# Layer one's experts in an AdaLN kernel: first products three tiles ahead instead of two

## The reference

```python
shared = silu(xf @ w_shared1) @ w_shared2
comb = zeros((T, 8)).at[arange(T)[:, None], top_k_idx].add(top_k_probs)
for e in range(8):
    expert_out = silu(xf @ w1[e]) @ w2[e]
    routed = routed + comb[:, e:e + 1] * expert_out
x = x + gb * (shared + routed)
```

## Time and profile before

| | |
|---|---|
| Median of 3 runs | 957.22 us (955.15 to 957.28) |
| The profiled execution's own time | 956.11 us |
| Its span, first to last instruction | 954.3 us |
| Instructions | 16734 |
| Busy: PE, DVE, ACT, POOL | 838.4, 791.0, 555.4, 463.9 us |
| Mean granted TensorE clock | 0.957 of 2.4 GHz |
| Stage `experts(1)` on PE | 861.46 to 948.6 us |

### The profile page before, as it was taken

One profiled execution on the slowest core, in us unless ns is written; L12 is line 12 of the kernel. 1 busy time (PEld: TensorE's weight loads), 2 busy tenths in 40 slices (PEclk: granted clock), 3 DMA queues, 4 the chain that ended last, 5 costly groups with the idle time before them and its releaser, 6 DMA issues. The chain is left out here.

```text
span 954.3 us, 16734 instructions
## 1 busy us (share of the span) xinstructions
PE 838.4 (88%) x5486; PEld 590.4 (62%) x5486; DVE 791.0 (83%) x1749; ACT 555.4 (58%) x1225; POOL 463.9 (49%) x459
## 2 busy tenths in 40 slices
PE   4778999999999999999999889989985785688897
PEld 3556677777677767777777667746553633345555
DVE  6978999999999999999888989786679878856752
ACT  3657877777778777777867667312123382552321
POOL 2146677676776655545544434545223122424652
PEclk9979999999999999999999999999997787899999
DMA  7013443343433432222333122422204113402122
GB/s 265 29 30 109 139 132 115 114 132 117 138 113 105 137 106 68 77 81 96 103 89 89 50 84 67 150 78 79 89 34 102 31 17 52 144 0 67 56 91 78
DMA packets 52662, 87.16 MB, mean 91 GB/s; under 512 B 5824, under 2 KB 23744, under 8 KB 51808
## 3 DMA queue, kind: packets, MB, share of 16 engines
q1 hardware_dynamic: 43360, 73.50, 26.0%
q10 hardware_dynamic: 9216, 12.59, 3.6%
HBM read 70.67 MB, written 15.40 MB: 90 GB/s over the span
## 5 line engine op out<-in xcount | busy, mean ns | idle before, releaser
L616 PE MATMUL bank<-hTs,wA 128*128 128x512 bf16 x768 | 180.1, 382 | 0.5 <-DVE u L1866 0.5
L2445 POOL TENSOR_TENSOR xbuf<-xbuf,dec 128x384 f32<-128x384 f32 x64 | 53.4, 834 | 211.7 <-ACT xbuf L1338 169.6
L1866 DVE SCALAR_TENSOR_TENSOR u<-bank,chn,u 128x511 f32<-128x511 f32 (+2 forms) x192 | 142.8, 744 | 3.5
L616 PEld LDWEIGHTS bank<-hTs,wA 128*128 128x128 bf16 x768 | 75.5, 99 | 83.4 <-issue 5.0
L688 PE MATMUL bank<-wB,yb 128*128 128x256 f32 x512 | 121.1, 380 | 0.7 <-DVE acc L1822 0.7
L688 PEld LDWEIGHTS bank<-wB,yb 128*128 128x128 f32 x512 | 92.5, 190 | 11.2 <-issue 1.1
L2455 POOL TENSOR_TENSOR yb<-yv,gs 128x512 f32<-128x512 f32 x64 | 81.8, 1277 | 14.1 <-DVE yv L1893 13.9
L767 PE MATMUL bank<-Mm,xbuf 128*128 128x128 f32 x512 | 71.8, 284 | 18.7 <-DVE yv L1893 17.5
L767 PEld LDWEIGHTS bank<-Mm,xbuf 128*128 128x128 f32 x512 | 65.9, 196 | 30.1 <-issue 21.2
L1348 ACT ACTIVATE rel<-csb,cs 128x128 f32<-128x128 f32 x256 | 82.4, 416 | 0.0
L1338 ACT ACTIVATE xbuf<-bank,dtv 128x128 f32<-128x128 f32 x256 | 72.8, 372 | 14.1 <-PE bank L733 14.1
(11 more groups left out here) (277 smaller groups left out, 1854.1 us busy)
## 6 DMA issues: line engine op xcount, KB each, us to landing
csb<-csd SPq DMA_DIRECT2D x64, 256.0 KB, 3.5
wA<-in_win SPq DMA_DIRECT2D x32, 256.0 KB, 4.4
wAd<-wA ACTq DMA_DIRECT2D x32, 256.0 KB, 4.4
wA<-wAd SPq DMA_DIRECT2D x32, 256.0 KB, 3.7
wB<-in_wob SPq DMA_DIRECT2D x8, 512.0 KB, 6.0
wBd<-wB ACTq DMA_DIRECT2D x32, 128.0 KB, 4.3
wB<-wBd SPq DMA_DIRECT2D x8, 512.0 KB, 5.5
sS<-cbd SPq DMA_DIRECT2D x16, 256.0 KB, 3.4
```

Of the source, the lines that this page charges most:

```text
L616: last = nc.tensor.matmul(out, wpart(a, kt), hpart(c, kt), start=n == 0, stop=n == 5)
L1866: nc.vector.scalar_tensor_tensor(out=u[:, n % 2, d:S], in0=bank[0][:, 0:S - d], scalar=chn[:, hid, 3 - d:4 - d], in1=u[:, n % 2, d:S], op0 ...
```

## The change

Layer one's tiles get a third PSUM bank (`UP[1]` = banks 0, 2, 3) and a third buffer for SiLU's result (`Ex[:, 0, 0:3]`, a tile of the attention, in place of two buffers in `words`). PE issues products(0), (1), (2) first, and products(m + 3) where it issued products(m + 2). PE's wait for a bank and ACT's wait for a buffer are for tile m - 3. The attention's leftovers move from bank 3 to bank 4, in all the places where bank pair (1, 3) stood. Layer zero's `UP[0]` = (0, 2) gives what stood there. POOL's and SP's lists are not touched.

```diff
-                         words[:, 0:2 * S].rearrange("p (f n) -> p f n", n=S),
+                         Ex[:, 0, 0:3, :],
...
+        UP = ((0, 2), (0, 2, 3))
...
                 def products(m):
                     b, pos, f = tile(L, m)
-                    if m > 1 and L:
-                        pe.wait_ge(q["fth_done"], tiles(1, m - 2))
+                    if m > 2 and L:
+                        pe.wait_ge(q["fth_done"], tiles(1, m - 3))
+                    elif L:
+                        pass
...
                     pe.wait_ge(q["fw_done"], (FT[0] if L else 0) + pos + 1)
                     for n in range(w13n):
-                        last = split_product(bank[2 * (m % 2) + n][:, :],
+                        last = split_product(bank[UP[L][m % len(UP[L])] + n][:, :],
...
                         for kt in range(KT):
-                            turned_heads(1, kt, bank[(1, 3)[kt]]).then_inc(q["a_attT"], 1)
+                            turned_heads(1, kt, bank[(1, 4)[kt]]).then_inc(q["a_attT"], 1)
...
-                products(1)
+                ahead = len(UP[L])
+                for m in range(1, ahead):
+                    products(m)
                 pe.wait_ge(q["zb_done"], L + 1)

                 for m in range(B * nf):
                     b, pos, _ = tile(L, m)
-                    if m + 2 < B * nf:
-                        if tile(L, m + 2)[0:2] == (1, 0):
+                    if m + ahead < B * nf:
+                        if tile(L, m + ahead)[0:2] == (1, 0):
                             pe.wait_ge(q["hts_done"], 8 if L == 0 else 12)
-                        products(m + 2)
+                        products(m + ahead)
                     (heads_ended if L else second_batch)(m)
...
                 def hidden(m):
                     b, pos, _ = tile(L, m)
-                    if m > 1:
-                        act.wait_ge(q["fh_done"], hidden_tiles(L, m - 2))
+                    ring = len(UP[L])
+                    if m >= ring:
+                        act.wait_ge(q["fh_done"], hidden_tiles(L, m - ring))
...
                     act.wait_ge(q["fu"], tiles(L, m))
-                    out = room[L].fth[:, m % 2, :]
+                    out = room[L].fth[:, m % ring, :]
...
-                    nc.scalar.activation(out, bank[2 * (m % 2)][:, :], ACT.Silu).then_inc(q["fth_done"], 1)
+                    nc.scalar.activation(out, bank[UP[L][m % ring]][:, :], ACT.Silu).then_inc(q["fth_done"], 1)
...
-                    nc.vector.tensor_tensor(room[L].hf[:, m % 3, :], room[L].fth[:, par, :], other, ALU.mult).then_inc(q["fh_done"], 1)
+                    nc.vector.tensor_tensor(room[L].hf[:, m % 3, :], room[L].fth[:, m % len(UP[L]), :], other, ALU.mult).then_inc(q["fh_done"], 1)
```

More of the change, by code:

```diff
@@ L894, in heads_ended @@
                             pe.wait_ge(q["a_attc"], KT)
-                            heads_out(1, half, bank[(1, 3)[half]]).then_inc(q["a_out"], 1)
+                            heads_out(1, half, bank[(1, 4)[half]]).then_inc(q["a_out"], 1)
                     if m == 7:
                         for ft in range(KT):
-                            turned_rows(3, 1, ft, bank[(1, 3)[ft]])
+                            turned_rows(3, 1, ft, bank[(1, 4)[ft]])
                     if m == 8:
@@ L1477, in experts @@
                             act.wait_ge(q["a_attT"], kt + 1)
-                            nc.scalar.activation(attT[1][:, kt, :], bank[(1, 3)[kt]][:, :], ACT.Copy)\
+                            nc.scalar.activation(attT[1][:, kt, :], bank[(1, 4)[kt]][:, :], ACT.Copy)\
                                 .then_inc(q["a_attc"], 1)
@@ L1481, in experts @@
                         for ft in range(KT):
-                            modulated(3, 1, 1, ft, bank[(1, 3)[ft]])
+                            modulated(3, 1, 1, ft, bank[(1, 4)[ft]])
                     if L and m == 9:
@@ L2098, in heads_ended @@
                             dve.wait_ge(q["a_out"], half + 1)
-                            last = gated_heads(1, half, bank[(1, 3)[half]])
+                            last = gated_heads(1, half, bank[(1, 4)[half]])
                         link(last)
```

## The result

| | before | changed |
|---|---|---|
| Median of 4 runs | 957.21 us | 967.05 us |
| Ratio, 95% interval | | 1.0099 (1.0064 to 1.0134) |
| Span of the profiled execution | 954.3 us | 967.4 us |
| Stage `experts(1)`: products(0) to DVE's first read of the last output | 861.46 to 948.67 = 87.2 us | 863.60 to 961.81 = 98.2 us |

One of the changed kernel's four runs took 1748.89 us; this outlier counts in the median and not in the ratio, and the other three took 964.32, 964.85 and 969.24 us. The kernel is slower by about 1%, 9.5 us by the ratio. Two more measurements of the same kernel beside the experiments gave 1.0122 (1.0086 to 1.0158) and 1.0122 (1.0084 to 1.0161), so the effect is 9.5 to 11.7 us. The prediction said slower, at 966.8 us. Of the 13.1 us between the two spans 11.0 lie in the stage; the other 2.1 lie ahead of it, where nothing was changed.

A forecast was written before the change was run, and what follows sets the result against it. The first batch was taken as bound by a chain through all engines, the second by PE's work. 8.8 us plus 0.8 for the clock, 9.6, gave 965.7 on the profiled 956.11, or 966.8 against the median; range 963.5 to 971.5.

The forecast's parts named there:

- the new wait: First batch, m = 0 to 9: products(m + 3) waits for POOL's input_rows(m + 3), made behind hidden_rows(m); some 12 us of waits.
- the term for the clock: PE's longer pauses bring one clock fall of 1.5 us, half of it on the chain: +0.8 us, bounds 0 and 4.5.
- 1, first turned weights: Tile 0: 0.3 us waiting for input_rows(3) and 1.29 of products(3) put the turned weights 1.6 us later.
- 2, heads_out: Tiles 2 and 3: input_rows(5), products(5), ACT's copies, SiLU(3), hidden_rows(3), input_rows(6), products(6) in series; heads_out 6.7 us later in all.
- 4, turned_rows: Tile 7: turned_rows needs products(10), which needs input_rows(10); 8.9 us later in all.
- 5, routes: Tiles 8, 9: routes, behind products(11) and input_rows(11), starts at 910.6 instead of 898.75; DVE waits for it, 9.4 us later.
- 6, second turned weights: Tiles 9 to 12: PE runs rows_out(8) to products(14) in one piece; second turned weights 10.2 us later, rows_out(12) 10.1.
- 7, end of the stage: Second batch: PE-bound as before, with one products fewer; 10.1 - 1.29 = 8.8 us later.
- third rival: Clock falls at each long pause of PE: three falls of 1.5 us on the path, 8.8 + 4.5, 970.5 us; chance 0.20.
- The rival that nothing changes: Whole stage: lead shifts 1.29 us in and out again, the wait for input_rows does not bite; 957.2 us, chance 0.06.
- the one by which the third bank fills PE's idle time: One more products covers the old waits of rows_out and products, 6.0 + 1.2 us; 950.0 us, chance 0.03.
- The short chain: DVE or ACT take SiLU(3) sooner, so only the heads_out delay counts: 6.7 - 1.29 = 5.4, 962.6 us; chance 0.11.

The follow-up runs named there:

- e8: Changed kernel with 35 extra matmuls on zeros ahead of products(4), (5), (6), (7) and (11), where PE waits for input_rows; ratio 1.0110, stage 96.0 us.
- e1: Changed kernel with POOL's input_rows one tile further ahead too, input_rows(m + 4) behind hidden_rows(m); 957.84 us, ratio 0.9999.
- e4: Changed kernel with SiLU of tile 3 ahead of the two copies of turned heads on ACT instead of behind them; 964.53 us, ratio 1.0111.
- e0: Changed kernel measured and profiled again, unaltered; 970.67 us, ratio 1.0122.
- e10: Changed kernel measured and profiled a third time, unaltered, beside e11; 967.01 us, ratio 1.0122.
- e5: e1 with the clearing and the first turned weights ahead of products(3) at tile 0; 954.82 us, ratio 0.9992.
- e6: e5 with the attention's leftovers ahead of products(m + 3) instead of behind it; 953.01 us, ratio 0.9972.
- e9: e6 with the clearing and the first turned weights ahead of products(2) as well as products(3); 950.25 us, ratio 0.9952.
- e3: Changed kernel with products(m + 3) moved behind rows_out(m) in layer one, so that PE's order is the old one; 958.35 us, ratio 1.0000.
- e7: Kernel before, two banks and a lead of two, with only the attention's leftovers ahead of products(m + 2); 952.81 us, ratio 0.9986.
- e2: Kernel before, two banks and a lead of two, with only POOL's input_rows one tile later; 970.08 us, ratio 1.0133.
- e11: The kernel of e4 measured again, on the same chip as e10; 963.82 us, ratio 1.0103.

## Why the prediction was right

The forecast was 966.8 us, with 963.5 to 971.5 as the range; the median came out at 967.05, and the three runs behind the ratio have a mean of 966.1. The forecast was right by its mechanism, the new wait. That the total came out so close is luck, since the term for the clock was too small. The steps can be read against two profiles, each as time since products(0) started, minus the same in the kernel before. The filled kernel (e8) is the changed one in an execution with the clock at 1.00 throughout, so it tests the steps without the clock.

| step | before, us in | predicted | changed | filled |
|---|---|---|---|---|
| 1, first turned weights | 4.33 | +1.6 | +1.7 | +1.7 |
| 2, heads_out | 15.60 | +6.7 | +8.3 | +6.9 |
| 4, turned_rows | 33.36 | +8.9 | +11.4 | +9.2 |
| 5, routes | 37.29 | +11.85 | +14.5 | +12.3 |
| 6, second turned weights | 48.82 | +10.2 | +12.7 | +10.4 |
| 7, end of the stage | 87.21 | +8.8 | +11.0 | +8.8 |

**The new wait** was right in mechanism and size. It went over POOL's list, which the diff does not touch: the change moved products past a signal that came just in time. The extra products shifts in and out at net zero (e1). **Step 2**, the dear one, held: SiLU(3) behind the copies costs what it was said to (e4, 2.1 us less for 2.3). The filled column is within 0.5 us of the predicted one at every step.

**The clock** is the term that was mis-sized. "One fall, with half of it on the chain", 0.8 us, was taken. Measured are 2.2, 3.7 and 6.0 us over the filled kernel's 96.0 in the three profiles, the last of them above the third rival's 4.5. Where they were lost follows from the same comparison, point by point: how much later than in the filled kernel, in us.

| stretch with the clock at 0.50 | first profile | e0 | e10 |
|---|---|---|---|
| the very start of the stage | none | 2.3 | none |
| rows_out(1) | 0.2 | none | 0.0 |
| products(6) and heads_out | 1.7 | none | 1.7 |
| products(7) and behind it | 0.3 | 0.0 | 0.0 |
| products(11), routes and behind them | none | 1.4 | 4.3 |

What failed is "one fall": inside the stage there were three, two and four, and the one in e10 at routes went on for ten us. The low clock at the very start is e0's alone among these three; e1, e5, e6 and e9, which have no such wait, show it as well, so this change need not have caused it. The reason given for counting half, "because long stretches of the chain run on DVE", held where it applies. While DVE's row work paces the chain, a slow stretch of PE cost 0.3 us at most: in the first profile PE worked without a pause from 896.20 until turned_rows at 908.36 and so used up waits that the filled kernel has there (0.19, 1.71 and 0.23 us). The dear ones lay where PE's own work is on the chain, at heads_out and at routes. In the first profile about 13.7 us at half clock took some 6.9 us from PE, and 2.2 of them, a third, reached the end.

So by its clock term the third rival, three falls and 4.5 us, was nearer than the forecast. The total was close because the first measurement gave 9.5 us; by all three it is 9.5 to 11.7, and two of the three are above the 9.6 that were summed. Even the highest, 1.0122 times 957.2 or 968.9 us, is inside the range.

The rule of the Trainium skill ("TensorE: Matmul & The Clock Gate", section "A second HAM failure mode: psum-queue depth-cycling") was nearer than I gave it credit for: idles between groups of matmuls make the clock swing. The runs narrow it. In the eight profiles in which PE, once the stage had started, never paused for more than 2.04 us, the clock did not fall inside the stage: the kernel before, e1, e3, e5, e6, e7, e8 and e9, among them e3 with its three banks in turn. In the other six, whose longest pauses are 3.28 to 3.55 us, it fell two to four times in five (the changed kernel's three, e2 with its two banks, and e11) and in e4 not at all; the first fall of the first profile followed a pause of 2.08 us. So in these profiles the falls go with the long pauses and not with the number of banks, and no pause is certain to bring one.

**Of the signs named in advance** the starts came true in the filled kernel, which starts the stage at 861.38 us as the old one does at 861.46: products(3) at 865.66, heads_out at 883.87, turned_rows at 903.94 and the second turned weights at 920.64, for 865.6, 883.8, 903.8 and 920.5. The changed kernel's own first profile is later by its later start (2.1 us) and by the clock. The sum of the waits came true too (12.3 us for "some 12"), but in six places and not ten: where PE came late by its low clock, input_rows was ready. The filled kernel and the old kernel with the wait have nine. The second batch ran without gaps.

The rival that nothing changes fell, and so did the one by which the third bank fills PE's idle time: even the free lead leaves those 6.0 us as they are (e1). The short chain, in which only step 2 counts, fell as well: steps 4 to 6 are there in the filled kernel.

## What to carry to other kernels

A step can only move ahead as far as every signal it waits on, those of just-in-time work in another engine's list included, so look where that work stands there before lengthening a lead. A uniform lead puts one more step ahead of the chain at the start and takes one off at the end, and fills no wait that is caused elsewhere; what pays is to take other work off the path ahead of the steps on which the chain hangs (leftovers ahead of products: 2.5 us off the stage). Pauses of two or three microseconds added to TensorE should be priced with the lower clock that can follow them, for each by whether TensorE's work behind it is on the chain.

## What the runs showed of the hardware

More work can come with a shorter stage: with useless matmuls in its waits, 7.5 us more of PE's work, the stage took 96.0 instead of 98.2 to 102.0 us, at a granted clock of 1.00 instead of 0.90 to 0.94. This is one execution. Without any filler one execution of e4 kept 1.00 from 866.5 to 956.5 us too, through pauses of 3.15, 3.18 and 3.29 us.

What a fall costs depends on where it lies: 0.0 to 0.3 us behind products(7), where another engine paces the chain, and 1.7 us at heads_out and 1.4 to 4.3 us at routes, where PE's work is on it.

Once low, the clock can stay low although TensorE is busy all the time: 8.00 of 8.00 us from 912 to 920 in the third profile of the changed kernel, where the earlier trace rows had shown a stretch of 3 us. I had taken three.

The same instructions ahead of the stage, but for bank numbers, took 853.9 to 864.0 us from one profiled execution to another. The low clock sat at the very start of the stage in eight of the fourteen and not in the other six. PE's pause just ahead of it does not tell them apart: it is 1.90 and 1.88 us in the kernel before and the first profile of the changed one, which started at 1.00, and 1.89 us in e4 and e11, which started at 0.50. What decides it in one execution was not tested. The 10 us of spread ahead of the stage are 1% of the time and hide an effect of 1 or 2 us, which the length of the one stage still shows.
